# The second output projection's bias is added to the residual on GpSimd, and VectorE adds products and residual in one instruction

## The chip, the core and the metric

One NeuronCore of a Trainium2 chip runs the whole program. The metric is the device time of one execution in microseconds (us), and the median of the runs counts. TensorE does the matmuls, VectorE, ScalarE and GpSimd the elementwise work, SyncE issues most of the DMAs. In the profile they are PE (PEld for its weight loads), DVE, ACT, POOL and SP.

## The reference, cut to what matters

Two transformer layers, each of attention and a feed-forward part, with a residual and a layer normalisation behind each of the four parts. The input is x, 2048 tokens of 128 features, float32.

```python
x = layernorm(x + attn0(x))     # causal, 8 heads of 128, 2 key-value groups through a latent of 32
x = layernorm(x + ffn0(x))      # silu-gated, 352 wide, operands quantised to FP4 in blocks of 16
x = layernorm(x + attn1(x))     # not causal, 16 heads of 8, 4 key-value groups
x = layernorm(x + moe1(x))      # 8 experts of 128x128, gate weights under 0.1 dropped

# attn1, with the part that the change is about in the last line
q = (x @ Wq.T + bq); k = (x @ Wk.T + bk); v = (x @ Wv.T + bv)
y = softmax(q k^T / sqrt(8)) v
return y @ Wo.T + bo            # so the third residual sum is x + y @ Wo.T + bo
```

## The kernel before, in words

**Tiling.** Tokens lie on the 128 partitions. X holds all 16 tiles of 128 tokens in SBUF (P x NT x D). Everything is done in four chunks of 512 tokens (QC = 512, QT = 4 tiles), and a product of a chunk fills one PSUM bank, 128 x 512 float32. There are eight banks; two take attention outputs, the rest go round between score tiles and "side" steps.

**The order.** The program is one list of steps, written by generators (`steps0` for the first layer's attention with everything that hangs on it, `steps1` for one chunk of the second attention with the experts of the chunk before it). Each engine walks this same list and picks out its own part, so each engine's queue has the order of the list. A step is a tuple whose first entry names its kind. The kinds that matter:

- `scores` and `products`: a score tile of attention (TensorE, L827 for layer 0, L831 for layer 1), its exponential into PR (ScalarE, L1059) and its product with V (TensorE, L850). In the first, causal layer the 128x128 block on the diagonal is clipped by GpSimd in between (`clip`, L1138).
- `max`: scores in the other orientation, query by key, for the row maxima (TensorE, L740 and L745, into a side bank; VectorE reduces it, L1315, or with the mask, L1312, and thereby frees the bank). They are made one or more iterations ahead of the attention that needs them. In the second layer there are 64 for each chunk and group.
- `norm1`, `x2T`, `k1` (four groups), `v1`: at the end of the first layer's feed-forward of a chunk, VectorE normalises into X (L1252), TensorE transposes X (L785), projects keys (L705) and values (L715). Key projections are split in high and low parts by ScalarE (L984, L985) and a subtraction on GpSimd (L1167); queries of the first layer-1 group likewise. Values are moved to V1 by VectorE with their bias (L1303), which frees the bank. X of the chunk, as `norm1` left it, is the residual of the second attention.
- `on1`, `y1`, `norm2`, `x3T`: behind the second attention of a chunk, the normalised outputs are transposed (L754) and multiplied with the output projection (TensorE, L762) into a bank; VectorE adds the bias (L1364), releases the bank (L1365), adds the residual (L1366), takes statistics (L1237, L1244, L1246); GpSimd forms the power -1/2 of the variance (`rstd`, L1130); VectorE normalises into R (L1252); TensorE transposes R (L788).
- `logits` to `final`: gate and experts of the chunk (TensorE L803, VectorE L1382, GpSimd sums L1145 and L1147), statistics, store. For the last chunk, `closing`, the steps stand one after the other with no attention beside them.

**Waits.** Semaphores carry all dependences. `released(k)` is the count of a side bank's semaphore when the k-th side step has left it. `link` lets VectorE wait for its own instruction before it goes on. `ld["attn1"]` counts the loads of the second attention's weights and biases, among them bo_b, the output bias repeated on all partitions (L1121). GpSimd issues all its DMAs at the start (L1107 to L1125) and then walks the list.

**Where y1 and v1 lie.** `y1` of chunks 0 to 2 is a few steps into the first iteration of the next chunk's attention, amid `max` steps of that iteration; `y1` of chunk 3 is in `closing`. `v1` of chunks 0 and 1 comes near the end of an iteration of the first attention, behind that iteration's last clip; `v1` of chunk 2 at the end of the last iteration of the first attention, also behind its last clip; `v1` of chunk 3 behind all first-layer work. In GpSimd's part of the list, the entry ahead of `v1` is the fourth `k1` for chunks 0, 1 and 3, and the last clip for chunk 2; the entry behind it is a `rstd` for chunks 0 and 1 and a query subtraction for chunks 2 and 3.

Of the kernel before, what the change touches and what calls it, by code (L numbers as in the profile page):

```python
# [18 lines left out]
P = 128  # L19
# [50 lines left out]
def build(nc, A):  # L70
# [3 lines left out]
    with ctx:  # L74
# [6 lines left out]
        def sem(name):  # L81
            return ctx.enter_context(nc.semaphore(name))
# [110 lines left out]
        score_full = sem("score_full")  # L193
        exp_done = sem("exp_done")
        pv_done = sem("pv_done")
        clipped = sem("clipped")
        out_free = sem("out_free")
        weights_ready = sem("weights_ready")
# [104 lines left out]
        def by_pool(item):  # L303

            return item[0] == "k1" or item[0] == "q1" and item[2] == 0
# [298 lines left out]
        def released(k):  # L604

            return freed_at[k]
# [482 lines left out]
        @block.gpsimd  # L1089
        def _(pool):  # L1090

            nc.gpsimd.memset(MS[:, :], 0.0).then_inc(pv_done, NP_RING)
            nc.gpsimd.memset(RS[:, :], 0.0).then_inc(side_free[0], 1)
            nc.gpsimd.memset(VE[:, :], 0.0).then_inc(side_free[1], 1)
            nc.gpsimd.memset(GS[:, :, :], 0.0).then_inc(side_free[2], 1)
            nc.gpsimd.memset(bq13[:, :, :], 0.0)
            nc.gpsimd.memset(bk13[:, :], 0.0)
            nc.gpsimd.memset(GM[:, :, :], 0.0).then_inc(summed, 2)
            pool.wait_ge(summed, 2)
            nc.gpsimd.memset(GW[:, :, :], 0.0).then_inc(side_free[3], 1)  # L1100
            pool.wait_ge(side_free[3], 1)
            nc.gpsimd.memset(G2[:, :, :], 0.0).then_inc(consts_set, 1)
            pool.wait_ge(consts_set, 1)
            nc.gpsimd.memset(KO0[SHIFT:KR, :, :].bitcast(f32), 1.0).then_inc(shifted, 64)
            pool.wait_ge(shifted, 64)
            nc.gpsimd.memset(UNUSED[:, :], 0.0).then_inc(ones_set, 1)
            pool.dma_start(Wq1[:, :], A["L1_attn_Wq"]).then_inc(ld["attn1"], 16)  # L1107
            pool.dma_start(Wo1[:, :], A["L1_attn_Wo"]).then_inc(ld["attn1"], 16)
            pool.dma_start(Wkv1[0:LAT, :], A["L1_attn_Wk"]).then_inc(ld["attn1"], 16)
            pool.dma_start(Wkv1[LAT:2 * LAT, :], A["L1_attn_Wv"]).then_inc(ld["attn1"], 16)  # L1110
            for band in range(2):
                for r in range(3):
                    rows = slice(band * BAND + r * HD1, band * BAND + (r + 1) * HD1)
                    for pair in range(PAIRS):
                        pool.dma_start(bq13[rows, pair, :],
                                     A["L1_attn_bq"].rearrange("(g h d) -> h d g", g=G1, h=HG)[2 * pair + band],
                                     allow_slow_non_contiguous=True).then_inc(ld["attn1"], 16)
                    pool.dma_start(bk13[rows, :], A["L1_attn_bk"].rearrange("(g d) -> d g", g=G1),
                                 allow_slow_non_contiguous=True).then_inc(ld["attn1"], 16)
            for dst, name, n in ((bv_b, "L1_attn_bv", LAT), (bo_b, "L1_attn_bo", D)):  # L1120
                pool.dma_start(dst[:, :], A[name].rearrange("(a n) -> a n", a=1).broadcast_to([P, n])).then_inc(ld["attn1"], 16)  # L1121
            pool.dma_start(gb_b[:, :], A["L1_ffn_gate_b"].rearrange("(a n) -> a n", a=1).broadcast_to([P, NE])).then_inc(ld["moe"], 16)
            pool.dma_start(gw[:, :], A["L1_ffn_gate_w"]).then_inc(ld["moe"], 16)
            pool.dma_start(ew[:, :, :], A["L1_ffn_expert_w"].rearrange("e k n -> k e n")).then_inc(ld["moe"], 16)
            pool.dma_start(eb[:, :], A["L1_ffn_expert_b"]).then_inc(ld["moe"], 16)  # L1125

            def rstd(n):

                pool.wait_ge(var_ready, n)
                nc.gpsimd.tensor_tensor(RS[:, :], VE[:, :], minus_half, ALU.pow).then_inc(rstd_ready, 1)  # L1130

            nothing = nc.gpsimd.to_reg(0.0)

            def clip(unit, q0):

                block = PR[:, unit % NP_RING, q0:q0 + P]
                pool.wait_ge(exp_done, unit + 5)
                nc.gpsimd.affine_select(block, block, [[1, P]], ALU.is_ge, nothing, base=0, channel_multiplier=-1).then_inc(clipped, 1)  # L1138

            def sum_experts(q, links):  # L1140

                t = TMP[q % 2]
                for w in (4, 2, 1):
                    links = links + 1
                    nc.gpsimd.tensor_tensor(t[:, 0:w, :], t[:, 0:w, :], t[:, w:2 * w, :], ALU.add).then_inc(pool_chain, 1)  # L1145
                    pool.wait_ge(pool_chain, links)
                nc.gpsimd.tensor_tensor(ACC[:, q, :], ACC[:, q, :], t[:, 0, :], ALU.add).then_inc(summed, 1)  # L1147
                return links

            def walk(steps, n, lag):  # L1150
                k, rs, tiles, tails, units = 0, 0, 0, 0, 0
                for step in steps:
                    kind = step[0]
                    if kind == "scores":
                        if diagonal(*step[1:3], step[5]):
                            clip(n.units + units, first_query(*step[1:3], step[5]))
                        units += 1
                    if kind in ("y0", "y1", "down", "stats"):
                        rs += 1
                        rstd(n.rstd + rs)  # L1160
                    if kind in ("expert", "ebias"):
                        last = k
                    if by_pool(step):

                        pool.wait_ge(*released(k))
                        dst = of_parts(step)[0]
                        nc.gpsimd.tensor_tensor(dst, WHOLE[tails % len(WHOLE)], dst.bitcast(f32),  # L1167
                                                ALU.subtract).then_inc(tailed, 1)
                        tails += 1
                    if kind == "sum":  # L1170

                        pool.wait_ge(*released(last))
                        sum_experts(step[1], 3 * (n.tiles + tiles))
                        tiles += 1
                    k += is_side(step)

            pool.wait_ge(ld["const"], 16)
            pool.wait_ge(ones_set, 1)
            parts(pool, walk)


        @block.vector
        def _(dve):
# [158 lines left out]
            def chunk_item(item, bank, tiles, free, n, cnt):  # L1342
# [15 lines left out]
                elif kind in ("y0", "down"):  # L1358
                    part = 1.0 if kind == "y0" else 0.5
                    link(v.scalar_tensor_tensor(R[:, :, :], tiles, part, chunk_of(item[1]), ALU.mult, ALU.add))  # L1360
                    v.engine_nop().then_inc(free, 1)
                    statistics(R)
                elif kind == "y1":
                    link(v.tensor_tensor(R[:, :, :], tiles, bo_b[:, :].unsqueeze(1).broadcast_to([P, QT, D]), ALU.add))  # L1364
                    v.engine_nop().then_inc(free, 1)  # L1365
                    link(v.tensor_tensor(R[:, :, :], R[:, :, :], chunk_of(item[1]), ALU.add))  # L1366
                    statistics(R)
                elif kind == "logits":
                    bc = lambda x: x.broadcast_to([P, QT, NE])
                    link(v.tensor_tensor(GL[:, :, :], bank[:, 0:QT * NE].rearrange("p (q e) -> p q e", e=NE),  # L1370
                                         gb_b[:, :].unsqueeze(1).broadcast_to([P, QT, NE]), ALU.add))
                    v.engine_nop().then_inc(free, 1)
                    link(v.tensor_reduce(GM[:, :, :], GL[:, :, :], AX, ALU.max))
                    v.tensor_tensor(GL[:, :, :], GL[:, :, :], bc(GM[:, :, :]), ALU.subtract).then_inc(logits_ready, 1)
                elif kind == "ebias":
                    v.tensor_tensor(ACC[:, :, :], tiles, R[:, :, :], ALU.add).then_inc(free, 1)  # L1376
                elif kind == "expert":
                    q, half, _ = item[1:]
                    if half == 0:

                        dve.wait_ge(summed, n.tiles + cnt.tiles + 1)
                    v.tensor_tensor(TMP[q % 2][:, 4 * half:4 * half + 4, :], tiles,  # L1382
                                    GW[:, q, 4 * half:4 * half + 4].unsqueeze(2).broadcast_to([P, 4, D]),
                                    ALU.mult).then_inc(free, 1)
# [152 lines left out]
```

## Time and profile before

| what | value |
|---|---|
| runs, us | 1390.56, 1385.19, 1389.36 |
| median, us | 1389.36 |
| the profiled execution's own time, us | 1391.06 |
| its span, first to last instruction, us | 1389.3 |
| TensorE's mean granted clock in it | 0.94 of full speed |
| GpSimd busy, us (share) | 141.0 (10%) |
| ScalarE busy, us (share) | 822.1 (59%) |

The first layer takes the first 600 us or so, the second attention runs from there to some 1357 us, and the last 32 us are what is left of the last chunk. The profile is of one execution. A busy time is the sum of an engine's instructions; a bracket such as [1.11 <-DVE MP L1315] at a row says that the engine stood idle for 1.11 us before that instruction and that VectorE's instruction of line 1315, writing MP, ended the idleness. Matmul ends are modelled, so TensorE's busy time doesn't mean that it works at its peak. An x4 merges four instructions in a row.

### The profile page before, as it was taken

Reading aid. Unit: us, or ns where it says so; the run is one execution under the profiler, and the core shown is the slowest. Engines: PE = TensorE matmul, PEld = TensorE weight load, DVE = VectorE, ACT = ScalarE, POOL = GpSimd, SP = SyncE. Lnnn points to the kernel's source line nnn. Section 1 sums busy time; section 2 is a strip of 40 time slices with the busy share of each in tenths; the row PEclk is TensorE's granted clock in tenths of the full one; section 3 lists DMA queues with packets and bytes.
Section 4 is the critical chain, followed back from the end, with each engine's and each line's share of the span. In section 5 each row is a group of like instructions: output and inputs, shape, how many; then the busy total and the mean of one; then the engine's idle time right before and its main releaser. Section 6 shows DMA issues by size and latency. Waiting matters only on the chain.

```text
span 1389.3 us, 19169 instructions
## 1 busy us (share of the span) xinstructions
PE 1263.5 (91%) x6358; PEld 555.3 (40%) x6358; DVE 1065.4 (77%) x2275; ACT 822.1 (59%) x1625; POOL 141.0 (10%) x259
## 2 busy tenths in 40 slices
PE   5689989999999954789999999999999999999895
PEld 3345445445443432433333443343343333334333
DVE  4667886898654558678898898999889999899524
ACT  3234436455555421178888666787666787678772
POOL 5110111103020120100000002000012000000030
PEclk8669989999999986689999999999999999999997
DMA  4010100010000000000000000000000000000000
GB/s 105 21 27 22 25 1 3 22 24 1 1 1 1 1 1 0 0 1 1 1 1 1 1 1 8 1 1 1 1 1 8 1 2 1 1 1 2 1 1 16
DMA packets 10740, 10.86 MB, mean 8 GB/s; under 512 B 2857, under 2 KB 7521, under 8 KB 10641
## 3 DMA queue, kind: packets, MB, share of 16 engines
q1 hardware_dynamic: 9632, 8.84, 2.6%
q0 software_dynamic: 1008, 0.79, 0.3%
q8 instruction: 51, 0.84, 0.3%
q14 instruction: 49, 0.39, 0.1%
HBM read 3.66 MB, written 1.05 MB: 3 GB/s over the span
## 4 chain that ended last, share of the span: by engine, by line
PE 70%; DVE 17%; ACT 5%; issue 5%; POOL 1%; SPq 1%; DMA 1%; DVEq 0%; POOLq 0%; ACTq 0%
PE ps L850 23%; PE ps L831 14%; PE ps L740 9%; DVE MP L1315 8%; PE ps L827 6%; PE ps L745 4%; ACT PR L1059 3%; PE ps L803 2%; PE ps L736 2%; PE ps L769 2%; PE ps L705 1%; DVE ps L1312 1%; PE ps L751 1%; PE ps L780 1%; DVE ST L1237 1%
## 5 line engine op out<-in xcount | busy, mean ns | idle before, releaser
L1059 ACT ACTIVATE PR<-ps 128x512 f32<-128x512 f32 (+2 forms) x1344 | 698.8, 586 | 381.7 <-PE ps L827 193.4
L1315 DVE TENSOR_REDUCE MP<-ps 128x1 f32<-128x512 f32 x1216 | 761.9, 683 | 118.1 <-PE ps L740 69.9
L850 PE MATMUL ps<-PR,V 128*32 128x512 f32 (+2 forms) x2688 | 433.7, 601 | 3.1 <-ACT OS L937 2.5
L740 PE MATMUL ps<-KO,Q 64*128 64x512 f32 x1024 | 379.9, 459 | 14.2 <-DVE MP L1315 7.3
L831 PE MATMUL ps<-Q,KO 64*128 64x512 f32 x1024 | 343.7, 446 | 10.2 <-DMA Q<-MR 6.0
L831 PEld LDWEIGHTS ps<-Q,KO 64*128 64x128 f32 x1024 | 160.2, 186 | 297.4 <-issue 128.4
L740 PEld LDWEIGHTS ps<-KO,Q 64*128 64x128 f32 x1024 | 170.4, 189 | 90.1 <-DVE MP L1315 35.9
L745 PE MATMUL ps<-KO,QO 96*128 96x512 f32 (+2 forms) x320 | 124.3, 436 | 23.0 <-DVE QO L1296 10.0
L827 PE MATMUL ps<-QO,KO 97*128 97x512 f32 (+3 forms) x320 | 140.3, 454 | 4.1 <-DMA QO<-MR 2.4
L850 PEld LDWEIGHTS ps<-PR,V 128*32 128x32 f32 (+1 forms) x2688 | 74.1, 115 | 128.2 <-issue 61.4
L827 PEld LDWEIGHTS ps<-QO,KO 97*128 97x128 f32 x320 | 61.0, 197 | 130.9 <-issue 80.3
L745 PEld LDWEIGHTS ps<-KO,QO 96*128 96x128 f32 x320 | 64.6, 210 | 43.2 <-issue 11.5
L1312 DVE CUSTOM_DVE_ANT_0 ps<-ps,mask_qk 128x128 f32<-128x128 f32 (+3 forms) x128 | 62.8, 493 | 18.0 <-PE ps L745 17.7
L1138 POOL TENSOR_SCALAR_AFFINE_SELECT PR<-PR 128x128 f32<-128x128 f32 x128 | 39.5, 310 | 331.4 <-ACT PR L1059 330.6
L1130 POOL TENSOR_TENSOR RS<-VE,const 128x4 f32<-128x4 f32 x16 | 16.2, 1013 | 554.4 <-DVE VE L1246 554.4
L1290 DVE SCALAR_TENSOR_TENSOR Q<-ps,bq,Q 128x512 fp32r<-128x512 f32 x24 | 18.0, 750 | 27.5 <-ACT Q L952 18.9
L736 PE MATMUL ps<-XT,WQ 128*128 128x512 f32 x64 | 35.2, 632 | 1.9 <-ACT PR L1059 1.7
L803 PE MATMUL ps<-ew,XQT 128*128 128x512 f32 x64 | 35.8, 658 | 0.0
L1145 POOL TENSOR_TENSOR qa<-qa 128x512 f32<-128x512 f32 (+2 forms) x18 | 14.8, 823 | 196.8 <-DVE XQ L1376 189.4
L937 ACT ACTIVATE HQT<-ps 128x256 f32<-128x256 f32 (+3 forms) x37 | 11.2, 350 | 33.5 <-PE ps L775 33.4
L775 PE MATMUL ps<-const,H 128*128 128x128 f32 (+1 forms) x48 | 9.8, 319 | 22.3 <-DVEq L1230 22.3
L751 PE MATMUL ps<-const,OS 128*128 128x128 f32 x128 | 20.7, 292 | 3.5 <-ACT OS L937 3.2
(211 smaller groups left out, 772.3 us busy)
## 6 DMA issues: line engine op xcount, KB each, us to landing
QO<-Q SPq DMA_DIRECT2D x72, 64.0 KB, 2.0
Q<-MR SPq DMA_DIRECT2D x64, 2.0 KB
result<-V SPq DMA_DIRECT2D x4, 256.0 KB, 2.3
H<-in_L_attn_wq SPq DMA_DIRECT2D x1, 512.0 KB, 3.4
HQT<-in_L_attn_wo SPq DMA_DIRECT2D x1, 512.0 KB, 5.8
ew<-in_L_ffn_expert_w POOLq DMA_DIRECT2D x1, 512.0 KB, 4.2
bq<-in_L_attn_bq POOLq DMA_DIRECT2D x12, 0.1 KB, 3.4
wd<-in_L_ffn_w_down SPq DMA_DIRECT2D x1, 176.0 KB, 4.8
```

What stands on the lines that cost most here:

```text
L736: last = nc.tensor.matmul(bank[:, :], WQ13[:, g, pair, :, :], XT[:, c * QC:(c + 1) * QC], start=True, stop=True)
L740: last = nc.tensor.matmul(bank[:, :], Q1[rows, buf, h // 2, q * P:(q + 1) * P], KO1[rows, g, kc * QC:(kc + 1) * QC], start=True, stop=True)
L745: last = nc.tensor.matmul(bank[:, 0:n], QO[0:SHIFT, buf, h, q * P:(q + 1) * P], KO0[0:SHIFT, g, kc * QC:kc * QC + n], start=True, stop=True)
L751: last = nc.tensor.transpose(bank[:, q * P:(q + 1) * P], OS[:, item[1] % 2, q * P:(q + 1) * P], ident)
L803: last = nc.tensor.matmul(bank[:, :], X2T[:, q * P:(q + 1) * P], ew[:, 4 * e:4 * e + 4, :], start=True, stop=True)
L827: m = nc.tensor.matmul(dst[:, q0:QC], KO0[:, g, kt * P:(kt + 1) * P], QO[:, buffer_of(0, it), h, q0:QC], start=True, stop=True)
L831: m = nc.tensor.matmul(dst[:, :], KO1[rows, g, kt * P:(kt + 1) * P], Q1[rows, it, h // 2, :], start=True, stop=True)
L850: nc.tensor.matmul(dst, VO[layer][:, kt, g, :], PR[:, u % NP_RING, q0:QC], start=kt == 0, stop=kt == key_tiles(layer, c) - 1).then_inc(pv_ ...
L1059: nc.scalar.activation(PR[:, u % NP_RING, q0:QC], ps[:, bank_of_score[u], q0:QC], ACT.Exp, scale=SCALE[layer]).then_inc(exp_done, 1)
L1138: nc.gpsimd.affine_select(block, block, [[1, P]], ALU.is_ge, nothing, base=0, channel_multiplier=-1).then_inc(clipped, 1)
L1312: v.tensor_tensor_reduce(bank[:, 0:w], bank[:, 0:w], mask_qk[:, QC - w:QC], 1.0, LOWEST, ALU.add, ALU.max, MP[:, buf, h, q, kc:kc + 1]).th ...
L1315: v.tensor_reduce(MP[:, buf, h, q, kc:kc + 1], bank[:, 0:w], AX, ALU.max).then_inc(free, 1)
```

## The change

GpSimd's walk gets a new branch: at each `v1` step it waits for the loads of the second attention and for the release of that step's bank, and then adds bo_b to the chunk of X in place, counted by a new semaphore. VectorE's `y1` waits for that count and adds bank and X into R in one instruction, in place of two.

```diff
@@ -193,6 +193,7 @@
         pv_done = sem("pv_done")
+        biased = sem("biased")
         clipped = sem("clipped")
@@ -1160,6 +1161,12 @@
                     if kind in ("expert", "ebias"):
                         last = k
+                    if kind == "v1":
+
+                        pool.wait_ge(ld["attn1"], N_ATTN1)
+                        pool.wait_ge(*released(k))
+                        x = X[:, step[1] * QT:(step[1] + 1) * QT, :]
+                        nc.gpsimd.tensor_tensor(x, x, bo_b[:, :].unsqueeze(1).broadcast_to([P, QT, D]), ALU.add).then_inc(biased, 1)
                     if by_pool(step):
@@ -1361,9 +1368,9 @@
                 elif kind == "y1":
-                    link(v.tensor_tensor(R[:, :, :], tiles, bo_b[:, :].unsqueeze(1).broadcast_to([P, QT, D]), ALU.add))
+                    dve.wait_ge(biased, item[1] + 1)
+                    link(v.tensor_tensor(R[:, :, :], tiles, chunk_of(item[1]), ALU.add))
                     v.engine_nop().then_inc(free, 1)
-                    link(v.tensor_tensor(R[:, :, :], R[:, :, :], chunk_of(item[1]), ALU.add))
                     statistics(R)
```

## Rows read from the trace of the kernel before

**Rows 1.** The page's busy times: us, share of the span, instructions.
```profile
PE 1263.5 (91%) x6358; PEld 555.3 (40%) x6358; DVE 1065.4 (77%) x2275; ACT 822.1 (59%) x1625; POOL 141.0 (10%) x259
```

**Rows 2.** The page's chain that ended last, shares of the span by engine.
```profile
PE 70%; DVE 17%; ACT 5%; issue 5%; POOL 1%; SPq 1%; DMA 1%; DVEq 0%; POOLq 0%; ACTq 0%
```

**Rows 3.** Busy time by stretch: a plain one, and the last.
```profile
core 0: us, PE busy (x) PEld busy (x) DVE busy (x) ACT busy (x) POOL busy (x), PEclk, DMA share, GB/s
...
870.00:980.00 110.00, 108.36 (x650) 43.79 (x648) 101.42 (x173) 86.01 (x168) 0.00 (x0) 1.00 0.00 1
...
1357.00:1389.30 32.30, 18.88 (x76) 11.98 (x76) 15.28 (x60) 6.42 (x20) 2.01 (x2) 0.78 0.06 17
```

**Rows 4.** VectorE's groups by form: shapes, count, busy us, mean ns, idle before.
```profile
L1360 DVE SCALAR_TENSOR_TENSOR R<-ps,X 128x512 f32<-128x512 f32 x8 | 5.5, 692 | 15.2 <-PE ps L758 5.9 <-PE ps L780 5.5 <-PE ps L745 2.1
...
L1364 DVE TENSOR_TENSOR R<-ps,bo_b 128x512 f32<-128x512 f32 x4 | 2.8, 692 | 4.5 <-PE ps L762 4.5
L1366 DVE TENSOR_TENSOR R<-R,X 128x512 f32<-128x512 f32 x4 | 2.8, 688 | 0.2
```

**Rows 5.** Timeline, first chunk's y1: start, us, engine, instruction, idle before.
```profile
780.60 0.69 DVE L1364 TENSOR_TENSOR R<-ps,bo_b 128x512 f32<-128x512 f32 x1 [0.17 <-PE ps L762]
781.34 0.69 DVE L1366 TENSOR_TENSOR R<-R,X 128x512 f32<-128x512 f32 x1
...
782.06 0.87 DVE L1237 BATCH_NORM_STATS2 ST<-R 128x6 f32<-128x128 f32 x4
...
784.21 0.49 PE L740 MATMUL ps<-KO,Q 64*128 64x512 f32 x1 [1.11 <-DVE MP L1315]
```

**Rows 6.** Timeline, last chunk's y1.
```profile
1360.54 0.69 DVE L1366 TENSOR_TENSOR R<-R,X 128x512 f32<-128x512 f32 x1
1361.26 0.87 DVE L1237 BATCH_NORM_STATS2 ST<-R 128x6 f32<-128x128 f32 x4
...
1365.11 1.11 PE L788 MATMUL ps<-const,R 128*128 128x128 f32 x4 [5.42 <-DVE R L1252]
```

**Rows 7.** Timeline, TensorE behind y1 of the second and third chunk.
```profile
986.36 0.49 PE L740 MATMUL ps<-KO,Q 64*128 64x512 f32 x1 [1.10 <-DVE MP L1315]
...
1188.95 0.50 PE L831 MATMUL ps<-Q,KO 64*128 64x512 f32 x1 [1.17 <-DVE MP L1315]
```

**Rows 8.** Busy time by stretch behind the three waits, columns as in rows 3.
```profile
784.20:797.40 13.20, 13.20 (x69) 5.51 (x69) 9.29 (x20) 7.16 (x14) 0.44 (x1) 0.87 0.00 1
986.30:998.30 12.00, 11.89 (x69) 5.22 (x69) 9.12 (x21) 7.13 (x14) 0.49 (x1) 1.00 0.00 1
...
1188.20:1196.30 8.10, 7.15 (x33) 2.62 (x33) 8.06 (x17) 4.07 (x8) 1.01 (x1) 0.79 0.00 0
```

**Rows 9.** Timeline, GpSimd and VectorE around v1 of chunks 0, 2 and 3.
```profile
215.78 1.29 POOL L1167 TENSOR_TENSOR KO<-wgu,KO 128x512 fp32r<-128x512 f32 x1
232.40 1.01 POOL L1130 TENSOR_TENSOR RS<-VE,const 128x4 f32<-128x4 f32 x1 [15.33 <-DVE VE L1246]
...
492.88 0.49 DVE L1303 TENSOR_TENSOR V<-ps,bv_b 128x32 f32<-128x32 f32 x4 [0.39 <-PE ps L715]
494.01 0.29 POOL L1138 TENSOR_SCALAR_AFFINE_SELECT PR<-PR 128x128 f32<-128x128 f32 x1
499.39 1.27 POOL L1167 TENSOR_TENSOR Q<-WHOLE,Q 128x512 fp32r<-128x512 f32 x1 [5.09 <-ACT Q L985]
...
581.79 8.46 DVE L1315 TENSOR_REDUCE MP<-ps 128x1 f32<-128x512 f32 x14
581.83 1.29 POOL L1167 TENSOR_TENSOR KO<-wgu,KO 128x512 fp32r<-128x512 f32 x1
...
604.58 1.28 POOL L1167 TENSOR_TENSOR Q<-WHOLE,Q 128x512 fp32r<-128x512 f32 x1 [21.45 <-ACT Q L985]
```

**Rows 10.** Timeline, two clips on GpSimd beside a VectorE multiply.
```profile
136.51 1.00 POOL L1138 TENSOR_SCALAR_AFFINE_SELECT PR<-PR 128x128 f32<-128x128 f32 x2 [7.74 <-ACT PR L1059]
...
136.93 0.42 DVE L1225 TENSOR_TENSOR XQ<-qa,qs 128x256 f32<-128x256 f32 x1
```

## The prediction

> **What bounds the kernel now.** I read the busy times first, then the chain that ended last, the stretches, and at the end the timeline around each instruction that the change touches. TensorE is busy for 91% of the span and VectorE for 77% [rows 1]; of the chain 70% is TensorE and 17% VectorE [rows 2]. So TensorE paces the whole, but VectorE isn't far behind: in the plain stretch of the second attention, 870 to 980 us, TensorE is busy 108.4 of 110 us and VectorE 101.4 [rows 3]. VectorE has there 8% in hand, and whatever it does besides its row maxima is paid from that. In the last 32 us the picture is another one: TensorE is busy 18.9 of 32.3 us, VectorE 15.3, ScalarE 6.4, and they take turns [rows 3]. The reader is to see in the rows that a VectorE instruction is free where TensorE is full, and is paid whole where the engines take turns or where TensorE runs dry. So the question is where the four pairs of adds of the second output projection lie.
>
> **What is removed.** Each of the four chunks has the pair: bank plus bias into R (692 ns), R plus X into R (688 ns) [rows 4]. The change leaves one instruction, bank plus X into R. The kernel has that operand pattern already, in the first attention's residual add, eight times at 692 ns [rows 4], so I cost the new one like the first of the pair. From the start of the second add to the start of the statistics is 782.06 - 781.34 = 0.72 us in the first chunk [rows 5] and 1361.26 - 1360.54 = 0.72 us in the last [rows 6]: the instruction and the hand-over behind it. Four of them are 2.9 us of VectorE. The release of the bank stays behind the first instruction, so it moves nowhere.
>
> **What of that lies on the path.** In the last chunk all of it. The statistics start at once when the second add ends, GpSimd's power follows, the normalisation, and TensorE has then been idle for 5.42 us waiting for R [rows 6]. This is 0.72 us off the end.
> In the first three chunks the pair lies amid row maxima, and these hold the banks that TensorE wants next. After the pair, the statistics and the first maximum, TensorE starts again at 784.21 us, having waited 1.11 us for a maximum [rows 5]; in the second chunk it waits 1.10 us at 986.36, in the third 1.17 us at 1188.95 [rows 7]. Each wait is longer than 0.72 us, so all of it can come off and 0.4 us of the wait is left. What is late next is TensorE itself: in the 12.0 us after the second chunk's wait it is busy 11.89 us and VectorE 9.12 [rows 8]. An engine that is full after a gap keeps what the shorter gap gave. So I take 3 x 0.72 = 2.2 us here; the bounds are 0 (all swallowed by a later wait) and 2.2.
>
> **What is added on VectorE.** One more wait in front of the remaining add, on a count that GpSimd reached hundreds of microseconds before. No row has that very wait; the nearest is the hand-over between the two adds, with a semaphore in it: 781.34 - (780.60 + 0.69) = 0.05 us [rows 5]. The bounds are 0, since it is long fulfilled, and 0.05. I take 0.05, four times 0.2 us. Behind it stand the statistics and the maxima; were GpSimd late, all of them would be. It isn't: see next.
>
> **What is added on GpSimd.** Four adds of 128x512, with X and a repeated bias row as inputs. GpSimd's nearest ones are its key subtractions of that size, 1.29 us [rows 9]; a bound below is 0.69 us, VectorE's for that size [rows 4], a bound above twice 1.29, since the repeated row has no row of its own on GpSimd. I take 1.29 us. Where they land: the step is the chunk's value projection, which follows the last of four key subtractions in GpSimd's order, and I set the four against the timeline. In the first chunk the last key subtraction ends at 215.78 + 1.29 = 217.07, and the second chunk lies the same way; in the third a clip of the diagonal stands ahead of the add and ends at 494.01 + 0.29 = 494.30; in the fourth the subtraction ends at 581.83 + 1.29 = 583.12 [rows 9]. GpSimd's next instruction is the power at 232.40, after 15.33 us of idleness (the second chunk's is alike); a query subtraction at 499.39 after 5.09; one at 604.58 after 21.45 [rows 9]. The shortest of these covers, 5.09 us, is nearly four times the add, and even twice 1.29 fits in. No clip and no DMA of GpSimd's queue stands behind an add inside these gaps; all its DMAs are issued at the start. Its wait is for VectorE's release of the value projection's bank. In the third chunk, the tightest, the value adds end at 492.88 + 0.49 = 493.37, before that clip does [rows 9], so this wait costs nothing. Cost on the path: 0. If the cover went, each add would be 1.29 us of a clip or of a query. Earliest use of the result is 780.60 us [rows 5], the last add's end some 584.4 us. X of a chunk is read between the two by no one.
>
> **A rule weighed.** GpSimd's clips take 0.29 us, as at 494.01 [rows 9]; but two of them at 136.51 took 1.00 us together, while VectorE ran an operation with two inputs in SBUF (L1225 at 136.93) [rows 10]. Beside row maxima, which read a bank, the subtractions at 215.78 and 581.83 took their usual 1.29 us, and no maximum is longer for it: fourteen in 8.46 us [rows 9]. The new adds will lie beside just such maxima. By the rows the sum gets nothing from this.
> The Trainium skill says in "SBUF — State Buffer", section "Who interferes with whom", that a VectorE instruction with two SBUF inputs contends with a GpSimd instruction that reads SBUF, and that the one that starts second is blocked until the other is done, while a reduction doesn't contend. By that rule the trace agrees, and the sum stays as it is as long as the adds lie beside maxima; where they met two-input work it would be the third rival below.
>
> **The sum.** Removed on the path 0.72 + 2.2 = 2.9 us, added 0.2: 2.7 us less. The profiled execution took 1391.06 us (a span of 1389.3 and 1.8 around it), so one like it would take 1388.4. The median of the runs before is 1389.36, which is 1.7 us under the profiled one; the forecast is 1389.36 - 2.7 = 1386.7 us.
>
> **First rival: swallowed.** The three inner chunks give nothing, because a later wait grows by as much: ScalarE's exponentials or a moved row of maxima could be what is late next. Then only the last 0.7 us stays, and the time is 1388.7. Against it: the rows behind the waits show TensorE full and nobody else [rows 8]. Chance 0.20.
>
> **Second rival: the clock.** The same 69 matmuls after the wait took 13.2 us in the first chunk, at a granted clock of 0.87, and 12.0 us in the second at 1.00 [rows 8], so a short fall from 2.4 to 1.2 GHz costs 1.2 us. Behind the third chunk's wait the clock was 0.79, and 0.78 in the last stretch [rows 3, 8]. Both came after an equal wait of 1.1 us, so a wait of 0.4 us may well have no such fall behind it, or it may have it elsewhere. If the falls behind the first and the third chunk go, and one near the last chunk, it is 3.6 us more: 1383.1. If one more comes, 1387.9. I give the first 0.08; the second is within the forecast's own range.
>
> **Third rival, slower: the engines block each other.** Place: the four adds on GpSimd. If its reads hold up VectorE after all, each add stops VectorE for up to 1.29 us, and behind VectorE stand the maxima that free TensorE's banks. Four of these are 5.2 us, less the 2.7: 1391.9 us. It decides from the point where each add holds the path for 2.7 / 4 = 0.68 us. Against it: the maxima beside subtractions keep their length [rows 9]. For it: the clips at 136.51 show that the two engines can block each other [rows 10]. Chance 0.05.
>
> That the change does less than it says can't be excluded by rows but by the code: the pair goes in every chunk, and the add is issued for every chunk.
>
> **The numbers.** Forecast 0.62, swallowed 0.20, clock 0.08, blocked 0.05; 0.05 is left for what no row shows. The likeliest time is 1386.7. The three runs before spread from 1385.19 to 1390.56, so a median can move by some 2 us by itself. The range reaches down to 1383.1, the clock rival, and up to the swallowed case's 1388.7 plus those 2 us, 1390.7. Half a percent is 6.9 us, about what a measurement of this kernel can tell from no change; faster by more than that needs less than 1382.4, beyond even the clock rival unless scatter helps: 0.05. Slower needs more than 1396.3, beyond the blocked case: 0.02. Within it: 0.93.
>
> **What would show it.** In the profile after: no second add, the statistics starting 0.05 us behind a first add of 0.69 us, 4 times; VectorE's busy time lower by 2.8 us and GpSimd's higher by 5.2; four GpSimd adds of about 1.29 us, three of them near 217, 494 and 583 us, and the powers and query subtractions behind them at the same distance from what releases them; TensorE's waits of 1.1 us at 784, 986 and 1189 down to 0.4. The prediction is wrong if these waits stay at 1.1 us, if maxima beside the adds take over 0.7 us, if an add ends after the next clip is ready, or if the time moves by over 7 us.

## The result, and the profile after

The changed kernel took 1393.76 us (median of 10 runs, 1391.2 to 1395.14), the kernel before 1389.2 us (10 runs, 1385.19 to 1390.92). The ratio is 1.0034, with a 95% interval from 1.0022 to 1.0046: slower by 4.6 us, where 2.7 us faster was forecast, and outside the range. It is within half a percent. Some executions of either kernel take 1381 to 1385 us at a higher mean clock and none of them was profiled, so a ratio, which takes in every run, need not be the ratio of two medians.

The profiled execution of the changed kernel took 1392.4 us. Its busy times, from the page (us, share, instructions), answer to [rows 1]:

```profile
PE 1267.5 (91%) x6358; PEld 556.3 (40%) x6358; DVE 1062.4 (76%) x2271; ACT 823.1 (59%) x1625; POOL 146.1 (11%) x263
```

VectorE has four instructions and 3.0 us less, GpSimd four instructions and 5.1 us more, as planned. But TensorE, which has the same 6358 matmuls, is busy 4.0 us longer. The groups by form show the two new instructions; GpSimd's add takes 1.28 us and starts at once behind what GpSimd did before (idle 0.0):

```profile
L1372 DVE TENSOR_TENSOR R<-ps,X 128x512 f32<-128x512 f32 x4 | 2.8, 692 | 4.5 <-PE ps L763 2.6 <-issue 1.5 <-DVE MP L1322 0.3
...
L1169 POOL TENSOR_TENSOR X<-X,bo_b 128x512 f32<-128x512 f32 x4 | 5.1, 1277 | 0.0
```

The timeline of the first chunk's y1, and TensorE behind the three waits, answer to [rows 5] and [rows 7] (start, us, instruction, idle before; every start is some 2.1 us earlier than in the profile before because of the first 60 us of the execution, ahead of anything that was changed):

```profile
778.47 0.69 DVE L1372 TENSOR_TENSOR R<-ps,X 128x512 f32<-128x512 f32 x1 [0.16 <-DVE MP L1322]
779.20 0.87 DVE L1244 BATCH_NORM_STATS2 ST<-R 128x6 f32<-128x128 f32 x4
...
781.34 0.50 PE L741 MATMUL ps<-KO,Q 64*128 64x512 f32 x1 [0.36 <-DVE MP L1322]
...
983.46 0.50 PE L741 MATMUL ps<-KO,Q 64*128 64x512 f32 x1 [0.36 <-DVE MP L1322]
...
1188.58 0.49 PE L832 MATMUL ps<-Q,KO 64*128 64x512 f32 x1 [0.41 <-DVE MP L1322]
```

The waits of 1.11, 1.10 and 1.17 us are 0.36, 0.36 and 0.41 us now. The work did at these places what the prediction said. The time was lost elsewhere. Busy time by stretch, before and then after, with the granted clock as the third figure from the right:

```profile
970.00:1180.00 210.00, 205.24 (x1166) 82.22 (x1162) 187.14 (x338) 150.99 (x290) 13.73 (x18) 1.00 0.01 2
1180.00:1300.00 120.00, 117.47 (x721) 47.44 (x724) 108.30 (x191) 94.16 (x182) 1.01 (x1) 0.99 0.01 1
1300.00:1357.00 57.00, 51.79 (x287) 17.38 (x286) 16.42 (x46) 41.26 (x81) 12.73 (x17) 0.97 0.00 1
```

```profile
970.00:1180.00 210.00, 206.31 (x1153) 82.19 (x1145) 184.09 (x332) 149.49 (x287) 13.74 (x18) 0.98 0.01 2
1180.00:1300.00 120.00, 117.35 (x725) 47.20 (x725) 108.34 (x190) 94.81 (x183) 1.01 (x1) 1.00 0.01 1
1300.00:1357.00 57.00, 52.96 (x282) 17.66 (x274) 14.49 (x39) 40.37 (x80) 12.24 (x17) 0.91 0.00 1
```

In 970 to 1180 the same 210 us hold 13 matmuls fewer at a clock of 0.98, and in the last attention stretch the clock is 0.91 where it was 0.97. A stretch at the lower clock is called a fall from here on. The trace's own list of clock stretches says where they are. Between the first score of the second attention (some 595 us) and the last chunk's output projection (some 1358 us) the kernel before was at the low clock, 1.2 GHz, at 785, 1191 and 1310 us for 3.4 us each. The changed kernel was at 789 (3.4 us), 991 (6.8), 1062 (3.4) and 1308 us (10.2). Here is the one at 991:

```profile
983.80:990.60 6.80, 6.78 (x43) 3.62 (x43) 6.72 (x14) 4.43 (x9) 0.09 (x1) 1.00 0.00 1
990.60:997.40 6.80, 6.80 (x19) 2.02 (x19) 1.59 (x5) 2.44 (x5) 0.00 (x0) 0.50 0.00 0
```

TensorE was busy 6.78 of 6.80 us, and then ran at half the clock for 6.8 us, in which 19 matmuls started instead of 43. The kernel before, with the longer wait, had no fall at this place [rows 8].

The fall at 1308 to 1310 us has a place of its own. In both kernels TensorE waits there for the row maxima that a DMA brings into Q, before and then after:

```profile
1309.40 0.73 PE L831 MATMUL ps<-Q,KO 64*128 64x512 f32 x4 [2.84 <-DMA Q<-MR]
```

```profile
1309.01 1.22 PE L832 MATMUL ps<-Q,KO 64*128 64x512 f32 x4 [2.84 <-DMA Q<-MR]
```

The wait is the same 2.84 us. In the kernel before the clock fell 0.8 us behind its end and stayed low for 3.4 us; in the changed kernel it fell 1.0 us ahead of its end and stayed low for 10.2 us. From the end of the wait to the last chunk's output projection it is 49.1 us before and 51.7 after, so 2.6 us of the loss lie behind this one wait.

**Theory.** The clock, by position: VectorE's shorter work moves the following matmuls by 0.7 us against whatever decides TensorE's clock, and another set of falls results. The falls cost the time; GpSimd's adds cost none. **Rivals.** GpSimd's adds cost it, by blocking or queueing; or each merged add costs something by itself; or work alone counts.

### The profile page after: what moved, and what is told of

Same layout as the page of the kernel before. It is cut to its first block, busy times and chain, and to the rows that moved or that the text cites. A ratio compares the mean times of both kernels' runs of the same rounds, so it can differ in the third digit from the quotient of the medians.

```text
span 1390.7 us, 19173 instructions
## 1 busy us (share of the span) xinstructions
PE 1267.5 (91%) x6358; PEld 556.3 (40%) x6358; DVE 1062.4 (76%) x2271; ACT 823.1 (59%) x1625; POOL 146.1 (11%) x263
## 4 chain that ended last, share of the span: by engine, by line
PE 69%; DVE 17%; ACT 5%; issue 5%; POOL 1%; SPq 1%; DMA 1%; DVEq 0%; POOLq 0%; ACTq 0%
PE ps L851 23%; PE ps L832 14%; PE ps L741 9%; DVE MP L1322 8%; PE ps L828 5%; PE ps L746 3%; ACT PR L1060 3%; PE ps L804 2%; PE ps L737 2%; PE ps L770 2%; DVE ps L1319 1%; PE ps L706 1%; PE ps L752 1%; PE ps L781 1%; DVE ST L1244 1%
## 5 line engine op out<-in xcount | busy, mean ns | idle before, releaser
L1322 DVE TENSOR_REDUCE MP<-ps 128x1 f32<-128x512 f32 x1216 | 762.0, 684 | 117.5 <-PE ps L741 69.9
L832 PE MATMUL ps<-Q,KO 64*128 64x512 f32 x1024 | 347.2, 448 | 10.2 <-DMA Q<-MR 6.0
L746 PEld LDWEIGHTS ps<-KO,QO 96*128 96x128 f32 x320 | 64.6, 210 | 42.7 <-issue 11.5
```

The lines of the kernel that those rows point to most:

```text
L746: last = nc.tensor.matmul(bank[:, 0:n], QO[0:SHIFT, buf, h, q * P:(q + 1) * P], KO0[0:SHIFT, g, kc * QC:kc * QC + n], start=True, stop=True)
L832: m = nc.tensor.matmul(dst[:, :], KO1[rows, g, kt * P:(kt + 1) * P], Q1[rows, it, h // 2, :], start=True, stop=True)
L1322: v.tensor_reduce(MP[:, buf, h, q, kc:kc + 1], bank[:, 0:w], AX, ALU.max).then_inc(free, 1)
```

## The experiments

Each kernel was timed in 3 or 5 rounds beside the kernel before on the same chip.

**1. VectorE's part alone** (the output bias is left out of the computation).

```diff
--- the changed kernel, without GpSimd's branch at v1
 elif kind == "y1":
-    dve.wait_ge(biased, item[1] + 1)
     link(v.tensor_tensor(R[:, :, :], tiles, chunk_of(item[1]), ALU.add))
```

> VectorE's part of the change alone: one add, bank plus X, and GpSimd adds nothing, so the output bias is left out of the computation. Theory (clock): the shorter VectorE work moves the second attention against TensorE's clock falls, and GpSimd's adds have no part in it, so this is 3 to 6 us slower than before, as the change is, with more time at the low clock between 600 and 1389 us than the 27 us of the profile before. Rival (GpSimd): the adds on GpSimd cost the time, so without them this is 2 to 3 us faster than before.

Measured: median 1392.77 us over 12 runs (1381.91 to 1394.69), before 1390.60; ratio 1.0000 (0.9982 to 1.0018). The loss of 3 to 6 us isn't clear in the ratio: nine runs lie at 1391.6 to 1394.7, three at 1381.9 to 1385.3. Its profile (1392.68 us) has 23.9 us of falls between the second attention's start and the last output projection, at 858, 991, 1192 and 1308 us. Without any work on GpSimd the falls are there; that this alone is slower isn't shown.

**2. GpSimd's part alone** (the bias is counted twice).

```diff
--- the changed kernel, with the pair of before
 elif kind == "y1":
     dve.wait_ge(biased, item[1] + 1)
-    link(v.tensor_tensor(R[:, :, :], tiles, chunk_of(item[1]), ALU.add))
+    link(v.tensor_tensor(R[:, :, :], tiles, bo_b[:, :].unsqueeze(1).broadcast_to([P, QT, D]), ALU.add))
     v.engine_nop().then_inc(free, 1)
+    link(v.tensor_tensor(R[:, :, :], R[:, :, :], chunk_of(item[1]), ALU.add))
```

> GpSimd's part alone: it adds the bias to X and VectorE waits for that, but VectorE keeps its pair of adds, so the bias is counted twice. Theory (clock): within 1.5 us of before, with the clock falls of before. Rival (GpSimd): slower than before by 7 us, what the change lost and the 2.7 us that it should have gained.

Measured: 1390.21 us, ratio 0.9993 (0.9984 to 1.0002). The falls of its profile stand at the same matmuls as those of the kernel before, and from 61 us to the end the starts of the matmuls keep the same distance in the two traces, 1.5 to 1.7 us. GpSimd's adds and the extra wait cost nothing. This rival is out.

**3. The last chunk alone.**

```diff
-if kind == "v1":
+if kind == "v1" and step[1] in (3,):
...
-elif kind == "y1":
-    dve.wait_ge(biased, item[1] + 1)
+elif kind == "y1" and item[1] in (3,):
+    dve.wait_ge(biased, (3,).index(item[1]) + 1)
```

(and the pair of before for the other chunks)

> The change in the last chunk alone; the first three keep the pair. Theory (clock): only the serial end is touched, so 0.7 us faster than before, give or take 1. Rival (GpSimd): a fourth of the loss, 1 us slower.

Measured: 1390.33 us, ratio 0.9998 (0.9989 to 1.0006), so too little to be seen in times. In the profile TensorE's wait for R behind the last y1 is 4.67 us, where run 2 has 5.41.

**4. The first three chunks** (the same with (0, 1, 2)).

> The change in the first three chunks, the last keeps the pair. Theory (clock): the falls come from the inner three, so 4 to 6 us slower than before. Rival (the last chunk is at fault): 2 us faster than before.

Measured: 1395.10 us, ratio 1.0029 (1.0016 to 1.0042), 4.0 us slower. The profile has the falls of run 1, 23.9 us of them. The loss comes with the inner three, where the work got shorter. The mean clock of the whole execution, which every run has, says the same: 0.941 in the fastest of the twelve runs (1387.22 us), 0.940 and 0.939 in the next two (1391.64 and 1391.83), 0.935 to 0.937 in the other nine (1394.39 to 1396.70).

**5 to 7. One chunk each**, with (0,), (1,) and (2,).

> The change in the first chunk alone (its y1 at 780 us). Theory (clock by position): 0.7 us of VectorE work less at one place moves all later work 0.7 us against the stretches where the clock falls, so the set of falls changes although nothing else is touched: the fall behind 784 us goes, others come further on, and the time moves by something other than -0.7 us, between -3 and +5. Rival (each merged add costs by itself what it lost): a third of the loss of the inner three, +1.3 us, with the new falls near 784 us only.

> The change in the second chunk alone (y1 at 983 us). Theory (clock by position): the work before 983 us as before, with the fall behind 784 us; behind 983 us another set of falls; time anywhere from -3 to +5 us. Rival (each merged add costs by itself): +1.3 us, new falls near 990 us only.

> The change in the third chunk alone (y1 at 1185 us). Theory (clock by position): falls as before up to 1185 us, and another set behind it, the one at 1190 us and the one at 1308 us above all; -3 to +5 us. Rival (each merged add costs by itself): +1.3 us, new falls near 1190 us only.

Measured on one chip, before 1392.09: first chunk 1390.39 us, ratio 0.9980 (0.9961 to 0.9999); second 1396.47, 1.0032 (1.0000 to 1.0063); third 1391.58, 0.9999 (0.9981 to 1.0018). By the middle of each ratio the same 0.7 us of saved work is a gain of 2.8 us in one place, a loss of 4.4 in the next, nothing in the third; the first two intervals only just end at 1, and the first still holds a gain of 0.7. The profiles are clearer: against the kernel before they have 3.5 us, 17.1 us and nothing more at the low clock, where run 4, with all three, has 13.7. The falls moved far from the edit: with the first chunk alone the fall at 785 goes, and new ones come at 859 and 985; with the second alone the last attention stretch, 300 us behind the edit, has 13.7 us of low clock where there were 3.4. Here it is, in the profile of the second chunk alone (columns as above):

```profile
1300.00:1357.00 57.00, 52.96 (x279) 17.56 (x271) 15.17 (x33) 39.96 (x79) 10.45 (x14) 0.88 0.00 1
```

That each merged add costs by itself, near its own place, is out: the first and the third chunk show no such cost.

**8. Three adds** (X is counted twice in the first three chunks).

```diff
     link(v.tensor_tensor(R[:, :, :], R[:, :, :], chunk_of(item[1]), ALU.add))
+    if item[1] < NC - 1:
+        link(v.tensor_tensor(R[:, :, :], R[:, :, :], chunk_of(item[1]), ALU.add))
```

> The kernel before with a third add of the same size in the y1 of the first three chunks, so VectorE works 0.7 us longer in each (X is added twice there). Theory (clock by position): the time isn't before plus 3 x 0.7 = 2.2 us, as it would be if only VectorE's work counted and was all on the path, but that sum and a different set of falls, so anything from -1 to +6 us, with falls that differ from those before. Rival (no clock effect, work only): +2.2 us, give or take 0.5, with the falls of before.

Measured: 1399.41 us, ratio 1.0047 (1.0031 to 1.0063), 6.5 us slower where the added work is 2.2. TensorE's waits behind the three y1 are 1.82, 1.82 and 1.88 us now, and the profile has 17.1 us more at the low clock than the kernel before. So less VectorE work was slower than before, and more was slower still.

**9 to 11. A pure delay.** The work stays, and starts later by n memsets of 0.9 us, at a place where TensorE runs dry.

```diff
     top = c + 1 if layer == 0 else NC
+    for _ in range(n if (layer, c, b) == (1, 0, 0) else 0):
+        link(v.memset(qc[:, 0:1024], 0.0))
     v.tensor_reduce(MS[:, :], MP[:, b, :, :, 0:top]...
```

> The changed kernel with a pure delay: one VectorE memset of 128x1024 (0.9 us) ahead of the first row maximum of the second attention, at about 590 us, where TensorE runs dry anyway. The work from there on is the same and starts some 0.4 to 0.9 us later. Theory (clock by position): the set of falls behind 780 us is another one than in the changed kernel, and the time moves by something other than +0.4 to +0.9, and can fall, by up to 4 us. Rival (work alone): +0.4 to +0.9 us against the change, same falls.

> The same with two memsets, 1.9 us. Theory (clock by position): another set of falls again; the three delays 0, 0.9 and 1.9 us don't lie on a line. Rival (work alone): +1.3 to +1.9 us against the change, on a line with the one before.

> The kernel before with the one memset. Theory (clock by position): the falls at 783 and 1189 us, which every profile of the kernel before's inner part showed, aren't where they were, and the time is off the line of +0.4 to +0.9 us, up or down by up to 4. Rival: +0.4 to +0.9 us, same falls.

Measured on one chip, before 1389.97: the changed kernel with one memset 1392.35 us, ratio 1.0020 (1.0004 to 1.0036); with two 1389.87, 1.0013 (0.9992 to 1.0034); the kernel before with one 1394.16, 1.0033 (1.0016 to 1.0050). Held against the 1.0034 of the result, the changed kernel doesn't get slower with the delay as work alone would have it; held against the 0.9990 that the same program has in run 13 below, it does, by 3 to 4 us. The times of the changed kernel so settle nothing here. The kernel before loses 4.6 us (ratio; at least 2.2 by the interval) to a delay of 0.9, which work alone doesn't explain. In the changed kernel with one memset, the falls at 789, 991 and 1062 us are gone; where it had half the clock, this one shows

```profile
984.00:997.40 13.40, 13.11 (x75) 5.69 (x74) 10.54 (x23) 8.52 (x17) 0.06 (x1) 1.00 0.00 1
```

75 matmuls in 13.4 us at the full clock, against 43 + 19 = 62 in the 13.6 us above.

**12. First and last chunk**, with (0, 3), the version that the runs pointed to.

> The change in the first and the last chunk, where it did not lose alone. Theory (clock by position): the falls of the run with the first chunk alone, and 0.6 us less at the end: 0.7 to 3.5 us faster than before. Rival (each merged add costs by itself): 1 to 2 us slower than before.

Measured: 1390.18 us, ratio 1.0000 (0.9981 to 1.0020). It doesn't beat the kernel before, against what was expected; the gain of the first chunk alone wasn't there on this chip. Its profile has the falls of that run, to 1 us.

**13 to 16. Averaging position out**, all on one further chip, before 1390.88.

> The changed kernel as it is, once more, on the same chip as the three others of this set. Theory (clock by position): 3 to 5 us slower than before, with falls near 789, 991, 1062 and 1308 us. If the loss isn't there on this chip, the theory of a fixed set of falls is wrong.

> The kernel before with two memsets (1.9 us) at 590 us. Theory: position alone decides the falls and the merged adds are worth 2.7 us at equal falls, so averaged over the delays 0, 0.9, 1.9 and 2.8 us the changed kernel is 1 to 3 us faster than the kernel before, though not at each. For this one: over 1391, since the changed kernel with the same delay had 1389.9. Rival (the change costs by itself, 4 us at any position): this one is near 1386.

> The kernel before with three memsets (2.8 us). Theory: see the run before; 1389 to 1396. Rival (the change costs by itself): 4 us under the changed kernel with the same delay.

> The changed kernel with three memsets (2.8 us). Theory: 1388 to 1395, and on the average over the four delays 1 to 3 us under the kernel before. Rival (the change costs by itself): 4 us over the kernel before with the same delay.

Measured:

| memsets | kernel before, ratio | changed kernel, ratio |
|---|---|---|
| 0 | 1 | 1.0034 (1.0022 to 1.0046); here 0.9990 (0.9973 to 1.0007) |
| 1 | 1.0033 (1.0016 to 1.0050) | 1.0020 (1.0004 to 1.0036) |
| 2 | 1.0040 (1.0027 to 1.0052) | 1.0013 (0.9992 to 1.0034) |
| 3 | 1.0018 (1.0005 to 1.0031) | 1.0016 (1.0004 to 1.0027) |

The mean over the four is 1.0023 for the kernel before and 1.0015 for the changed one (1.0012 taken for its two runs without a memset): 1 us less, at the low edge of what was expected and less than the intervals can tell. A cost of 4 us at every position is out. One expectation fell: on this chip the changed kernel, the same program as in the result, isn't slower (median 1390.99 us against 1390.88), and its profile has 17.1 us of falls, at 858, 1059 and 1305 us, where the first profile has 23.9. A program doesn't have one set of falls. The mean clock of the whole execution goes with this: mostly 0.939 in run 13, 0.935 to 0.937 in nine of the result's ten runs. The last attention stretch, for one, is at the same 0.91:

```profile
1300.00:1357.00 57.00, 51.41 (x267) 17.17 (x263) 13.40 (x40) 38.02 (x75) 12.74 (x17) 0.91 0.01 4
```

**What the profiles give together.** For each kernel the table has, from the trace, the time from the first score of the second attention to the last chunk's output projection, and the low-clock time in between (with what is left of the fall that is on at its start):

| kernel | stretch, us | low clock in it, us |
|---|---|---|
| before | 761.9 | 13.8 |
| GpSimd alone; last chunk alone | 762.0; 762.0 | 13.8; 13.8 |
| before with 1, 2, 3 memsets | 764.2; 763.4; 761.8 | 19.5; 18.3; 13.7 |
| changed | 766.2 | 27.5 |
| changed, run 13 | 762.8 | 20.7 |
| VectorE alone; first three chunks | 766.1; 766.1 | 27.5; 27.5 |
| changed with 1, 2, 3 memsets | 761.7; 760.4; 762.1 | 16.1; 11.5; 17.1 |

A straight line through the six profiles with the pair in the inner chunks has a slope of 0.38 us for each us at the low clock, one through the seven with three merged adds 0.37, and lies 1.0 us lower. So a fall of 3.4 us costs 1.3 us, the inner three merged adds are worth some 1 us together, and the first profiles' difference is 0.37 x (27.5 - 13.8) - 1.0 = 4.1 us, where 766.2 - 761.9 = 4.3 was measured. The thirteen lie within 0.6 us of their lines. The five profiles left out, runs 5 to 8 and 12, lie up to 1.3 us off the first line (first chunk alone: 762.2 us with 17.3 at the low clock; third alone: 762.5 with 13.8; three adds: 769.7 with 30.9). So a cause of a microsecond could still hide here, one of four couldn't. (The two spans differ by 1.4 us only, since the changed kernel's profile was 2.2 us ahead when the stretch began, and its end is 0.8 us shorter.)

**The wait at 1308 us in all eighteen profiles.** The wait for the DMA ends between 1305 and 1316 us and is 2.84 or 2.85 us in each. What differs is when the clock falls, counted from the end of that wait, and what follows:

| profiles | the clock falls, us from the wait's end | low for, us | from the wait's end to the last output projection, us |
|---|---|---|---|
| second chunk alone | -1.4 | 13.7 | 53.0 |
| changed (result; run 13; one memset), VectorE alone, first three chunks | -1.1 to -0.7 | 10.2 | 51.6 to 51.8 |
| the other twelve, with the changed kernel with two and with three memsets among them | -0.1 to +0.8 | 3.4 | 49.1 |

Here the theory can be read off directly: the same wait, met by the clock's fall up to 2.2 us earlier or later, is followed by 3.4, 10.2 or 13.7 us at the low clock. The 6.8 us more cost 2.5 to 2.7 us, which is the slope found above. It isn't the merged adds that make the fall long, since two and three memsets put the changed kernel into the short group.

## Why the prediction was wrong

**The accounts of work.** Four VectorE instructions gone, their place, the hand-over, GpSimd's add (1.28 us for 1.29 forecast), its cover and its zero cost (run 2): right. Three of the four adds sat beside row maxima as said, the third beside no VectorE work at all, and nothing blocked: the adds took 1.26 to 1.29 us, and three maxima beside the second one 1.89 us. The rival of blocked engines is out. The Trainium skill's rule in "SBUF — State Buffer", section "Who interferes with whom", that a reduction doesn't contend with GpSimd, agrees with this. The wait's cost, taken as 0.05 us, can't be seen. In the last chunk the statistics start 1362.70 - 1361.96 = 0.74 us behind the add's start, and the 0.7 us came off:

```profile
1361.96 0.69 DVE L1372 TENSOR_TENSOR R<-ps,X 128x512 f32<-128x512 f32 x1 [2.65 <-PE ps L763]
1362.70 0.87 DVE L1244 BATCH_NORM_STATS2 ST<-R 128x6 f32<-128x128 f32 x4
```

**The term of 3 x 0.72 = 2.2 us** was mis-sized: 1.0 us is what stayed. "An engine that is full after a gap keeps what the shorter gap gave" was true at the gap and not for long. GpSimd alone, and then the first chunk alone, 150 us behind the first y1, TensorE's timeline:

```profile
935.61 0.49 PE L832 MATMUL ps<-Q,KO 64*128 64x512 f32 x1
...
937.04 0.50 PE L741 MATMUL ps<-KO,Q 64*128 64x512 f32 x1
```

```profile
934.86 0.49 PE L832 MATMUL ps<-Q,KO 64*128 64x512 f32 x1
...
936.65 0.50 PE L741 MATMUL ps<-KO,Q 64*128 64x512 f32 x1
```

The first pair of matmuls is 0.75 us apart, the second, the same work 1.4 to 1.8 us on, 0.39: between them TensorE's weight loads wait for row maxima with the first chunk's add merged,

```profile
936.05 0.18 PEld L741 LDWEIGHTS ps<-KO,Q 64*128 64x128 f32 x1 [0.41 <-DVE MP L1322]
```

and 0.36 us of the lead is spent. So the swallowed rival was half right.

**The step that failed** is the clock. The prediction had the price of a fall (1.2 us; 1.3 measured), and saw that equal waits had a fall behind one and none behind the other [rows 8]. From that it gave a shorter wait the chance of fewer falls only, put one fall more at 1.2 us "within the forecast's own range", and took nothing for the clock into its sum. Two things were wrong. The falls don't go with these waits alone: the one at 991 came directly behind 6.8 us of a busy TensorE, and half of the 13.7 us more at the low clock lies at the wait of 1308 us, which the change doesn't touch. And it isn't a matter of one fall: an edit of 0.7 us in one chunk changed the set for hundreds of us behind it, with the second chunk alone by 17 us of low clock (30.9 us in its stretch), and the stretch took 768.0 us for 761.9. The second attention of the kernel before had three falls in 760 us, so there was room for many more, and a few of them at 1.2 us each belonged on the upper side of the range. In the two profiles of the result the missing term is 0.37 x 13.7 = 5.1 us, against 0.7 and 1.0 us saved: 3.4 us slower in all, where the two profiles differ by 3.6 behind the start of the second attention. The medians differ by 4.6; the rest lies in runs that weren't profiled. The 0.93 for a result within half a percent was right, as far as one result can say.

**What stays open.** What makes the clock fall at one place and not at another, with the same matmuls around it, wasn't found; no run changed TensorE's own order. At the wait of 1308 us the length of the fall goes with the position, in all eighteen profiles. Elsewhere it can't be all: the two profiles of the changed kernel have the same program in the same position and other falls. Nor is it shown whether the change gains or loses over many chips: the ratio was 1.0034 in the result and 0.9990 in run 13.

## What to carry to other kernels

Where TensorE's clock falls now and then in a kernel that keeps TensorE full, a saving of a few us is smaller than what the falls do when the work moves by 0.7 us. Price the low-clock time of the profile (here 0.37 us a us), compare kernels at equal low-clock time, and put the difference of the clock on both sides of the range. Look first at the waits that stand in every profile, such as the DMA wait of 2.84 us here: the low clock there can last three or four times as long without a change of the wait. A pure delay, put where the engines run dry and tried at several lengths, tells a cost of the work from one of position.

## What the runs showed of the hardware

**Position against the clock is the same from run to run.** In twelve profiles of kernels without memsets (runs 1 to 8, 12 and 13, and both kernels of the result), the clock rose 3.58 to 3.64 us behind the first score of the second attention, though that first score came at times up to 2.2 us apart. With one, two and three memsets it was 5.83, 4.63 and 3.45 us, for the kernel before and the changed one alike, to 0.02 us. The Trainium skill says in "TensorE: Matmul & The Clock Gate", "Part 1: The HAM clock gate", that the window in which activity is watched is free-running and isn't reset when a kernel starts. Read by itself, that would let the position vary from run to run; these traces show one position for all kernels that are alike up to 590 us. Something in the first 600 us, where the clock is low for some 140 us, may bring them into step; no run here shows what.

**The same position doesn't give the same falls.** The two profiles of the changed kernel had the rise at 3.60 and 3.59 us, and falls at 789, 991, 1062, 1308 against 858, 1059, 1305.

**No long wait is needed for a fall.** Ahead of the falls at 785 and 1191 us of the kernel before TensorE was busy 5.47 and 5.43 of 6.80 us, and ahead of the one at 991 of the changed kernel 6.78.

**The price.** The Trainium skill, in "TensorE: Matmul & The Clock Gate", section "Terms", puts the penalty of throttled time at roughly that time times one minus the granted share, here one half. By that rule 13.7 us more would be 6.9 us, an estimate; the runs show 0.37, 5.1 us. That part of the slower matmuls lies beside waits for other engines would explain it; no run shows it. Single falls differ: the first chunk alone gained 0.8 us on run 2 where the fall at 783 was gone, and lost 0.9 where the one at 858 came.
